# Attention sums and residual additions as identity products on TensorE, value products on GpSimd, and a hinted loop branch

## The reference

```python
# pad to 626 frames of 128, multiply by an orthonormal DCT: h is (32, 626, 128)
h = tok(x)
h = h + mamba_pair(layernorm(h))   # stage 1: two state-space scans (forward, backward), projection, layernorm
h = h + moe(layernorm(h))          # stage 2: 8 experts 128 -> 512 -> 128, the best 2 for each token
h = h + attn(layernorm(h))         # stage 3
h = h + patterns(layernorm(h))     # stage 4

# stage 3, for each of 128 channels and each position s, over a window of 8 positions:
logits = (q[s + w] + pos[w]) * k[s]          # w = 0..7, none past the end
attn = softmax(logits, over w)
out[s] = sum_w attn[w] * v[s + w]

# stage 4, for each token:
a1 = gelu(x @ input_patterns.T);  keep the 64 largest of 512
a2 = gelu(a1 @ process_input_weights.T);  keep the 128 largest of 256, softmax over them
a3 = gelu((a2 @ process_values) @ output_input_weights.T);  keep the 64 largest of 512
out = a3 @ output_patterns
```

## Time and profile before

| | us |
|---|---|
| median of 3 runs | 8,142.36 |
| lowest, highest | 8,140.66, 8,146.43 |
| the profiled execution's own time | 8,142.98 |
| its span, first to last instruction | 8,141.2 |

### The profile page before, as it was taken

One profiled execution on the slowest core, in us unless ns is written; L12 is line 12 of the kernel. 1 busy time (PEld: TensorE's weight loads), 2 busy tenths in 40 slices (PEclk: granted clock), 3 DMA queues, 4 the chain that ended last, 5 costly groups with the idle time before them and its releaser, 6 DMA issues.

```text
span 8141.2 us, 109594 instructions
## 1 busy us (share of the span) xinstructions
PE 5529.4 (68%) x31240; PEld 4441.6 (55%) x31240; DVE 6959.1 (85%) x22124; ACT 3232.6 (40%) x7204; POOL 3040.7 (37%) x3192
## 2 busy tenths in 40 slices
PE   6766677776667767667767667767667767667433
PEld 5655555555555555556555556555556555556322
DVE  2378989888989888989888989888989888989887
ACT  2343444433444443344443344433344443344311
POOL 2344443334443433443333443333443333443320
PEclk8887788878788888788877788878788878778755
DMA  2322222222222222222221222222222222222200
GB/s 71 107 79 62 66 85 78 74 65 60 65 85 79 78 62 61 62 85 81 79 64 57 62 84 82 80 62 62 64 77 82 81 65 65 67 67 82 69 2 3
DMA packets 342763, 561.90 MB, mean 69 GB/s; under 512 B 33728, under 2 KB 261792, under 8 KB 341664
## 3 DMA queue, kind: packets, MB, share of 16 engines
q10 hardware_dynamic: 152576, 357.68, 14.2%
q1 hardware_dynamic: 168992, 153.83, 7.3%
q0 software_dynamic: 20480, 41.98, 1.7%
HBM read 484.63 MB, written 68.74 MB: 68 GB/s over the span
## 4 chain that ended last, share of the span: by engine, by line
DVE 67%; PE 9%; issue 8%; DMA 5%; POOL 5%; ACT 3%; ACTq 2%; SPq 1%; DVEq 0%; POOLq 0%
DVE m L1218 15%; DVE work L1221 9%; DVE work L1251 7%; DVE sorted L1248 6%; DVE a L1221 4%; DVE ab L1071 3%; DMA rows<-routed_rows 3%; DVE lg L1173 2%; PE pS L565 2%; PE pD L761 2%; DVE Mt L1082 2%; DMA decay_rows<-dAT 2%; POOL u L387 2%; DVE stats L1030 2%; DVE red L1188 2%
## 5 line engine op out<-in xcount | busy, mean ns | idle before, releaser
L1218 DVE MAX8 m<-work 128x8 f32<-128x512 f32 x1792 | 1143.4, 678 | 1.0
L1221 DVE MATCH_REPLACE8 work<-m,work 128x512 f32<-128x512 f32 x1536 | 1024.8, 674 | 0.0
L565 PE MATMUL pS<-u_fm,wconv_s 128*128 128x315 f32 x3072 | 929.0, 457 | 6.1 <-ACT Cs L849 5.8
L674 PE MATMUL pM<-turned,expert 128*128 128x128 f32 x4352 | 655.2, 297 | 331.7 <-ACT turned L920 327.4
L674 PEld LDWEIGHTS pM<-turned,expert 128*128 128x128 f32 x4352 | 586.0, 206 | 423.6 <-issue 359.9
L565 PEld LDWEIGHTS pS<-u_fm,wconv_s 128*128 128x128 f32 x3072 | 614.2, 205 | 256.3 <-issue 52.8
L907 ACT ACTIVATE hid<-pM,expert 128x128 f32<-128x128 f32 x2176 | 621.2, 370 | 331.6 <-PE pM L674 330.2
L459 POOL TENSOR_TENSOR lg<-lg,red 128x640 f32<-128x640 f32 x256 | 388.5, 1557 | 920.2 <-DVE red L1179 920.2
L685 PE MATMUL pM<-expert,hid 128*128 128x128 f32 x4352 | 672.9, 306 | 0.0
L685 PEld LDWEIGHTS pM<-expert,hid 128*128 128x128 f32 x4352 | 631.6, 223 | 0.0
L599 PE MATMUL pS<-Mt,Xw 121*64 121x121 f32 x3072 | 294.2, 321 | 488.7 <-DVE Mt L1082 486.4
(11 more groups left out here) (243 smaller groups left out, 13975.1 us busy)
## 6 DMA issues: line engine op xcount, KB each, us to landing
expert<-in_experts ACTq DMA_DIRECT2D x544, 578.0 KB, 3.9
ab<-decay_rows SPq DMA_DIRECT2D x384, 230.7 KB
rows<-routed_rows SPq DMA_DIRECT2D x128, 256.0 KB, 5.1
answer_rows<-turned ACTq DMA_DIRECT2D x256, 128.0 KB, 4.0
x_sb<-in_x SPq DMA_DIRECT2D x32, 256.0 KB
out<-hk SPq DMA_DIRECT2D x32, 256.0 KB
routed_rows<-un,slot POOLq DMA_INDIRECT x320, 2.8
rows<-answer_rows,slot POOLq DMA_INDIRECT x320, 2.6
```

What stands on the lines that cost most here:

```text
L565: last = nc.tensor.matmul(pS[:, 512 * (n % 3):512 * (n % 3) + HQ], wt, tap(d, i, half * HQ, HQ), start=(j == 0), stop=(j == len(blocks) - 1))
L674: last = nc.tensor.matmul(pM[:, bank(i) + j * P:bank(i) + (j + 1) * P], w1_of(i, j), turned[:, (i + 2) % 4, 1, :], start=True, stop=True)
L1218: link(nc.vector.max(m8[:, i, :], now[i]), len(tiles) - 1)
L1221: link(nc.vector.match_replace(work[i], m8[:, i, :], now[i], GONE), len(tiles) - 1)
```

## The change

- **Denominator.** The seven additions on GpSimd go. TensorE forms the sum of the eight rows of `lg` as eight products with the identity matrix that accumulate in `pA`, in two halves of 320 positions. ScalarE copies each half to `q`. VectorE's reciprocal works on `q`.
- **Value products.** All eight are made by GpSimd: four into `red`, and after TensorE has read `lg` for the denominator, four in place. VectorE's four go.
- **Value sum.** The seven additions on GpSimd go. TensorE sums the eight rows the same way, in two halves, and VectorE multiplies each half of `pA` by the reciprocal.
- **Residual additions.** For h3, an ordinary product with the identity takes the place of the transpose, and a second identity product adds h3 to it; ScalarE copies the sum to h3. For the output, a fifth product with the identity adds `hk` in PSUM; ScalarE copies the result to `hk`. VectorE's additions go.
- **Branch.** The loop is made with `hint_back_edge=True` for each engine.
- **Orders.** All five strings are new. On VectorE the projections' scans are mixed with the pair rounds, the logits come after the last pair round instead of before the first, and the last layernorm of stage 1 comes before the third layer's end. On GpSimd the gathers come directly ahead of the normalization of h3, on the sync queue the loads of the first gathered rows come ahead of the first four decay loads, and on TensorE the first turned rows come behind three of the second layer's products.

```diff
-PE_ORDER = ("14444143433323231111111111214141411134411111111111122424322112211114111111114111112242222122211221211221"
-            "114221111111112114211411112444241414112241111211144142114221412112244144143414434433")
-ACT_ORDER = ("44414334413233121111111113114141421111111111341111424223242112111111111111112424222224224422132221241212"
-             "14424214442144424122144244122421221114424144433")
-DVE_ORDER = ("34244414244211114442444444444434444444411111144444444441111111111433111411114444144444444434444441414343"
-             "42")
-POOL_ORDER = ("321421333333331121113314")
-
-
-SP_ORDER = ("1112221111111213443")
+PE_ORDER = ("44414122114111211311141141113111414441311311141111311121241214212111111211121111342111121111114111112121"
+            "1112111112111211111112311111422311121122444442444242222242423224242434422234443343444433")
+ACT_ORDER = ("44144121211411111411131114113144141111131141131124111322411211121111214112421312142141422112211223111122"
+             "31124244444444244242222422324222432444243224244334444433")
+DVE_ORDER = ("342414424142141142444444444414414444141114111441111111411114111414444444341444414444444344344344342")
+POOL_ORDER = ("21312111313323131")
+
+
+SP_ORDER = ("1121111111211224")
 
...
-            with engine.Fori(last, NB) as b:
+            with nc.Fori(last, NB, engines=[engine.engine], hint_back_edge=True) as b:
...
-            for w in range(4):
-                last = nc.gpsimd.tensor_tensor(red[:, w, :], lg[:, w, :], lg[:, w + 4, :], ALU.add)
-            last.then_inc(G["den_tree"].s, 1)
-            yield
-            pool.wait_ge(G["den_tree"].s, G["den_tree"](b, 1))
-            for w in range(2):
-                last = nc.gpsimd.tensor_tensor(red[:, w, :], red[:, w, :], red[:, w + 2, :], ALU.add)
-            last.then_inc(G["den_tree"].s, 1)
-            yield
-            pool.wait_ge(G["den_tree"].s, G["den_tree"](b, 2))
-            nc.gpsimd.tensor_tensor(red[:, 0, :], red[:, 0, :], red[:, 1, :], ALU.add).then_inc(G["den_done"].s, 1)
-
-            yield
-            pool.wait_ge(G["den_done"].s, G["den_done"](b, 1))
+            for w in range(AW // 2):
+                last = nc.gpsimd.tensor_tensor(red[:, w, :], lg[:, w, :], v[:, w:w + W], ALU.mult)
+            last.then_inc(G["weighted"].s, 1)
+            yield
+            pool.wait_ge(G["den_ps"].s, G["den_ps"](b, 2))
             for w in range(AW // 2, AW):
                 last = nc.gpsimd.tensor_tensor(lg[:, w, :], lg[:, w, :], v[:, w:w + W], ALU.mult)
-            last.then_inc(G["val_tree"].s, 1)
-
-            for j, n in enumerate((4, 2, 1)):
-                yield
-                if j == 0:
-                    pool.wait_ge(G["weighted"].s, G["weighted"](b, 1))
-                pool.wait_ge(G["val_tree"].s, G["val_tree"](b, j + 1))
-                for w in range(n):
-                    last = nc.gpsimd.tensor_tensor(lg[:, w, :], lg[:, w, :], lg[:, w + n, :], ALU.add)
-                last.then_inc(G["val_tree"].s, 1)
+            last.then_inc(G["weighted"].s, 1)
             yield
             normalized(pool, 2, 2, b, u3, h3).then_inc(G["u4_done"].s, 1)
             yield
...
-            yield
-            pe.wait_ge(G["att_done"].s, G["att_done"](b, 1))
-            pe.wait_ge(G["qkv_sb"].s, G["qkv_sb"](b, 6))
+            for half in range(2):
+                yield
+                if half == 0:
+                    pe.wait_ge(G["lg_exp"].s, G["lg_exp"](b, 1))
+                    pe.wait_ge(G["qkv_sb"].s, G["qkv_sb"](b, 6))
+                else:
+                    pe.wait_ge(G["den_sb"].s, G["den_sb"](b, 1))
+                lo = W // 2 * half
+                for w in range(AW):
+                    last = nc.tensor.matmul(pA[:, 0:W // 2], ident, lg[:, w, lo:lo + W // 2], start=(w == 0), stop=(w == AW - 1))
+                last.then_inc(G["den_ps"].s, 1)
+            for half in range(2):
+                yield
+                if half == 0:
+                    pe.wait_ge(G["den_sb"].s, G["den_sb"](b, 2))
+                    pe.wait_ge(G["weighted"].s, G["weighted"](b, 2))
+                else:
+                    pe.wait_ge(G["att_done"].s, G["att_done"](b, 1))
+                lo = W // 2 * half
+                for w in range(AW):
+                    part = red[:, w, lo:lo + W // 2] if w < AW // 2 else lg[:, w, lo:lo + W // 2]
+                    last = nc.tensor.matmul(pA[:, 0:W // 2], ident, part, start=(w == 0), stop=(w == AW - 1))
+                last.then_inc(G["val_ps"].s, 1)
+            yield
+            pe.wait_ge(G["att_done"].s, G["att_done"](b, 2))
             for t in range(4):
-                last = nc.tensor.transpose(pA[:, tok(t)], att[:, tok(t)], ident)
+                nc.tensor.matmul(pA[:, tok(t)], att[:, tok(t)], ident, start=True, stop=False)
+                last = nc.tensor.matmul(pA[:, tok(t)], ident, h3[:, t, :], start=False, stop=True)
             last.then_inc(G["attT_ps"].s, 1)
             yield
             pe.wait_ge(G["h3_done"].s, G["h3_done"](b, 1))
-            nc.tensor.transpose(pA[:, 0:P], att[:, tok(4)], ident).then_inc(G["attT_ps"].s, 1)
+            nc.tensor.matmul(pA[:, 0:P], att[:, tok(4)], ident, start=True, stop=False)
+            nc.tensor.matmul(pA[:, 0:P], ident, h3[:, 4, :], start=False, stop=True).then_inc(G["attT_ps"].s, 1)
             yield
...
+                if t == 0:
+                    pe.wait_ge(G["h3_kept"].s, G["h3_kept"](b, 1))
                 for j in range(4):
-                    last = nc.tensor.matmul(pD[:, 512:512 + P], selT[:, j * P:(j + 1) * P], c("op")[:, j * P:(j + 1) * P],
-                                            start=(j == 0), stop=(j == 3))
-                last.then_inc(G["fin_ps"].s, 1)
+                    nc.tensor.matmul(pD[:, 512:512 + P], selT[:, j * P:(j + 1) * P], c("op")[:, j * P:(j + 1) * P],
+                                     start=(j == 0), stop=False)
+                nc.tensor.matmul(pD[:, 512:512 + P], ident, hk[:, t, :], start=False, stop=True).then_inc(G["fin_ps"].s, 1)
         @block.tensor
...
+            for half in range(2):
+                yield
+                act.wait_ge(G["den_ps"].s, G["den_ps"](b, half + 1))
+                lo = W // 2 * half
+                nc.scalar.copy(q[:, lo:lo + W // 2], pA[:, 0:W // 2]).then_inc(G["den_sb"].s, 1)
+            for n, (lo, hi) in enumerate(((0, 4 * P), (4 * P, W))):
+                yield
+                act.wait_ge(G["attT_ps"].s, G["attT_ps"](b, n + 1))
+                nc.scalar.copy(h3[:].rearrange("p t d -> p (t d)")[:, lo:hi], pA[:, 0:hi - lo]).then_inc(G["h3_done"].s, 1)
...
+                yield
+                act.wait_ge(G["fin_ps"].s, G["fin_ps"](b, t + 1))
+                nc.scalar.copy(hk[:, t, :], pD[:, 512:512 + P]).then_inc(G["out_sb"].s, 1)
...
-            dve.wait_ge(G["den_tree"].s, G["den_tree"](b, 1))
-            for w in range(AW // 2):
-                last = nc.vector.tensor_tensor(lg[:, w, :], lg[:, w, :], v[:, w:w + W], ALU.mult)
-            last.then_inc(G["weighted"].s, 1)
-            yield
-            dve.wait_ge(G["den_done"].s, G["den_done"](b, 1))
-            link(nc.vector.reciprocal(red[:, 1, :], red[:, 0, :]))
-            yield
-            dve.wait_ge(G["val_tree"].s, G["val_tree"](b, 4))
-            nc.vector.tensor_tensor(att[:], lg[:, 0, :], red[:, 1, :], ALU.mult).then_inc(G["att_done"].s, 1)
-            yield
-            dve.wait_ge(G["attT_ps"].s, G["attT_ps"](b, 1))
-            nc.vector.tensor_tensor(h3[:, 0:4, :].rearrange("p t d -> p (t d)"), h3[:, 0:4, :].rearrange("p t d -> p (t d)"), pA[:, 0:4 * P],
-                                    ALU.add).then_inc(G["h3_done"].s, 1)
-            yield
-            dve.wait_ge(G["attT_ps"].s, G["attT_ps"](b, 2))
-            nc.vector.tensor_tensor(h3[:, 4, :], h3[:, 4, :], pA[:, 0:P], ALU.add).then_inc(G["h3_done"].s, 1)
+            dve.wait_ge(G["den_sb"].s, G["den_sb"](b, 2))
+            nc.vector.reciprocal(q[:, 0:W], q[:, 0:W]).then_inc(G["den_done"].s, 1)
+            for half in range(2):
+                yield
+                dve.wait_ge(G["den_done"].s, G["den_done"](b, 1))
+                dve.wait_ge(G["val_ps"].s, G["val_ps"](b, half + 1))
+                lo = W // 2 * half
+                nc.vector.tensor_tensor(att[:, lo:lo + W // 2], pA[:, 0:W // 2], q[:, lo:lo + W // 2], ALU.mult).then_inc(G["att_done"].s, 1)
+            yield
             dve.wait_ge(G["h3_done"].s, G["h3_done"](b, 2))
...
-            due = []
             for tiles in groups:
                 yield
                 dve.wait_ge(G["a3_sb"].s, G["a3_sb"](b, tiles[-1] + 1))
-                for r, _ in enumerate(take_top(tiles, a1, K3, places(0))):
-                    yield
-                    if due and r % 2 == 1:
-                        if due[0] == 0:
-                            yield
-                            dve.wait_ge(G["h3_kept"].s, G["h3_kept"](b, 1))
-                        yield from out(due.pop(0))
```

(12 more changed lines are left out.)

## The result

The changed kernel takes 8,032.66 us (median of 4 runs, 7,998.63 to 8,044.30), the kernel before 8,141.51 us beside it (4 runs): a ratio of 0.986 (95% interval 0.983 to 0.989). I had predicted 7,940 with a range of 7,670 to 8,160. So the direction holds and the gain is about half of the forecast one: 109 us instead of 202. The time lies inside that range, but outside the forecast's own part of it (7,850 to 8,000).

A forecast was written before the change was run, and what follows sets the result against it. VectorE's work plus waits bounds the kernel: 211.9 + 3.2 small gaps + 0.4 + 10.2 + 10.3 = 236.0 us a pass against 242.7. With 16 us saved outside the loop that gives 7,933, stated as 7,940, range 7,670 to 8,160.

The forecast's parts named there:

- VectorE's work: VectorE's busy time in a pass: 6.23 us removed, 1.06 added, so 5.2 less, giving 211.9; bounds 4.5 to 5.5.
- The loop's edge: VectorE's wait at the first statistics behind the backward branch: the hint cuts it from 3.9 us to 0.4.
- the rival that the hint does nothing: The branch hint has no effect: 3.5 us more a pass, 239.5, kernel 8,034 us; chance 0.10.
- The projection stage: VectorE's waits from the pair split to the third layer's first group: 10.2 us a pass, bounds 0 to 14.
- the GELU: VectorE's wait at the pair split for the second layer's third GELU on ScalarE: 4.5 us instead of 8.1.
- the first weigh step: VectorE's first product on inputs TensorE has turned for the scan, after four of eight pair rounds: wait 4.0 us.
- later scan steps: VectorE's waits at the scan steps after the first: 0.7 us a pass, where the old order had 2.0.
- the third layer's first group: VectorE's wait at the first round of the third layer: 1 us a pass.
- The tail: VectorE's wait ahead of the expert sum at a pass's end: 10.3 us instead of 8.1, bounds 6.5 to 19.
- TensorE and GpSimd: Work moved a pass: TensorE rises to some 189 us, its sums taking 17.1 at full clock; GpSimd loses some 15.5.
- rival 2: TensorE runs the attention's sums at 1.2 GHz, expert sum 8.2 us later than forecast; 8,171 us; chance 0.14.
- Rival 1: The walk overstates ScalarE; the projection stage's wait is 2 us, not 10.2; pass 227.8, kernel 7,695 us; chance 0.27.

The follow-up runs named there:

- group 1: Four kernels on one chip; the kernel before with only the branch hint took 8,409.94 us (ratio 0.988), the changed kernel without the hint 8,411.07 (0.987).
- the kernel with all of it: Changed kernel with earlier end of a pass, GELU step moved ahead, third layer freed and six table loads fewer: 7,635.46 us, 0.951 of the changed kernel.

## Why the prediction was right in direction and too high in size

**VectorE's work**: forecast 211.9 a pass, measured 209.85. The instructions came as counted: 5.2 of work for each of 32 items is 166 of the 211.6 us. Some 36 of the rest are the scans, which took 485.1 us (384 of 1,270 ns) and now 448.6 (1,168 ns). They follow the order: 1,272 with the hint alone, 1,242 with the old orders, 1,168 in every kernel with the new ones, where GpSimd has nothing to do beside them in the pass shown. I had not costed this; some 9 us of the 211.6 I did not place.

**The loop's edge**: 0.4 forecast, nothing left. Right, and the rival that the hint does nothing (0.10) fell in group 1, although its time, 8,034, is the one that was measured. That is luck: the right time by the wrong mechanism.

**The projection stage**: this term was mis-sized, 10.2 forecast against 5.5 + 7.0 + 3.6 = 16.1, and 5.9 a pass is more than the whole shortfall. By its parts: the GELU 4.5 against 5.5; the first weigh step 4.0 against 6.3; later scan steps 0.7 and 0.7; the third layer's first group 1 against 3.6. The causes given for the first two held: ScalarE's order and its table loads. I had the loads at the right price (1.28), and two errors of my walk can be named. For the GELU, the parts that I list for ScalarE come to 21.0 and not to 20.0; with that the walk gives 28 and a wait of 5.3, and the trace has 28.3 for ScalarE (from the selected tile at 4140.2 to the third GELU's end at 4168.5) and 5.5. For the weigh step, VectorE took the 14.2 forecast from the pair split on, but ScalarE took 19.7 (4168.5 to 4188.2) where I had 18: there are seven table loads between, not six, and in the same stretch ScalarE stands 2.96 for the first expert tile's product, in 8 us with a granted clock of 0.60. TensorE's product adds 0.8, which I left out. Fewer loads took 5.0 from this wait, more than the whole 4.0 that I had given it. The third part is a step that I did not walk at all. I gave it 1 without a row. Its chain is in the timeline above: an expert tile's copy (4247.50) ahead of the first turned weights on ScalarE, its product (2.05 at half clock) ahead of the first aggregate on TensorE. Moving two steps took off 115 us.

**The tail**: 10.3 forecast, 10.1 measured, released as forecast by the kept copy and behind it by the transfer to the output. The size was right and the reading of it incomplete: three ends lay close together there, gathers, attention and output, and making the gathers early and freeing the kept copy of the transfer gave only 64 of the 150 us expected.

**TensorE and GpSimd**: 189 forecast, 190.15 busy; GpSimd 15.5 less forecast, 17.8 measured. The attention's four sums took 18.9 us of it an item (301.9, 154.0 and 148.3 us over 32 items) against 17.1 at full clock and 34 at half, so they ran at full clock for the most part (in the pass shown the granted clock is 1.00 in all four), and rival 2 fell.

**Rival 1** (the slack is real, 7,695, chance 0.27) was wrong for this kernel, and its time was not out of reach: with the orders mended and one more buffer the same work takes 7,635. TensorE at 76% and ScalarE at 45% did have the room. What they lacked was the right next step in their queues.

**The sum.** The loop saves 2.7 a pass in the mean instead of 6.7, 29 x 4.0 = 116; outside it 20 were saved instead of 16. 116 less 4 is 112, and from 7,933 to the profiled 8,044.3 it is 111.

## What to carry to other kernels

When one engine's work is cut in a kernel with hand-written orders, look at once at what it will wait for, step by step in the other engines' queues; here 7.3 us of work saved in a pass turned into 7.9 us of waits, and nine moved steps and one more buffer took off 391 us where the whole change had taken 114. A wait of a stage that was never walked is not 1 us: find what stands ahead of its first step in each queue. Where several chains end together, moving one of them can show little: the earlier gathers gave 64 us of the 150 that their wait promised. That more comes when the others are moved too is likely from the kernel with all of it, but not shown for this place alone.

## What the hardware showed that I had not expected

The hint on the loop's branch takes 3.6 us from each pass (105 us over 29 passes, in the kernel before) and halves the bytes of one instruction queue (3.31 to 1.71 MB). Three chips gave the kernel before 8,140, 8,463 and 8,515 us, at mean granted clocks of 0.80, 0.78 and 0.78; the changed kernel spread less, 8,026 and 8,203 on the first two. With the hint alone, on the third chip, the wait for a2 was 322.4 us over the run against 239.9 in the profile of the kernel before, and that for the output norm's mean 162.6 against 50.5. I read this as the clock, since both waits end short chains through TensorE, whose products took 5,691 us against 5,529; no run changes the clock alone. A scan of VectorE took 2.14 us instead of 1.17 in the one place of that pass where GpSimd was adding 640 columns beside it (kernel before, at 4301.56, in GpSimd's run of 11.54 from 4296.63); the Trainium skill, SBUF — State Buffer, section SBUF: two separate sides, says that an operation of VectorE with two inputs in SBUF and one of GpSimd that reads SBUF exclude each other, and this row agrees. It is not every time the scan that is held: beside GpSimd's four products, from 4275.60 in the same pass, three scans took 1.17, 1.34 and 1.22. Those products took 7.47, and four of them in the changed kernel 5.61 and 5.75. A table load takes 1.28 us, and the next operation starts 1.30 after it began (4243.58 and 4244.88 in the timeline above). The Trainium skill, ScalarE: Activation LUTs, section What ACT_TABLE_LOAD costs, gives 1.28 us for the load and 1.38 more for a drain; no drain is seen here, and the smaller price is the one to use for this kernel.
